# Relative attention of an eight-layer kernel: heads in pairs, values weighed in column strips, the mask inside the row maximum

## The reference

```python
q, k, v = (split_head(xn @ W) for W in (Wq, Wk, Wv))          # 16 heads of 8
scores  = q @ k^T / sqrt(8) + skew(q @ rel_embed^T)           # 512 x 512 a head
scores  = where(causal, scores, -inf)
out     = softmax(scores) @ v                                 # 512 x 8 a head
y       = merge_heads(out) @ Wp + bp
```

## Time and profile before

| | us |
|---|---|
| median of 3 runs | 4825.27 |
| lowest, highest | 4806.19, 4838.93 |
| profiled execution | 4821.89 |
| its span, first to last instruction | 4820.2 |

### The profile page before, as it was taken

How to read it: one execution, slowest core, us unless ns; L and a number is a source line. 1 busy time by engine, 2 the same in 40 slices (tenths; PEclk the granted TensorE clock), 3 DMA queues, 4 the chain that set the end, 5 groups by cost and what they waited for, 6 DMA issues and landing times.

```text
span 4820.2 us, 76474 instructions
## 1 busy us (share of the span) xinstructions
PE 4323.8 (90%) x30051; PEld 2656.8 (55%) x30051; DVE 2385.6 (49%) x6922; ACT 1718.7 (36%) x3496; POOL 841.7 (17%) x1441
## 2 busy tenths in 40 slices
PE   7988989889898898988989889898898988988989
PEld 3556645565455654556545565455654556545575
DVE  3435644365443654436544365443654446544455
ACT  2333533334333343333433334333343333433334
POOL 2003111031110311103011040110401104011140
PEclk8999999999899999999989999999998999999989
DMA  2000000000000000000000000000000000000000
GB/s 70 1 1 1 1 6 1 1 1 1 6 1 1 1 1 6 1 1 1 1 6 1 1 1 1 6 1 1 2 1 6 1 1 2 1 4 1 1 1 3
DMA packets 19714, 17.25 MB, mean 4 GB/s; under 512 B 2605, under 2 KB 18942, under 8 KB 19326
## 3 DMA queue, kind: packets, MB, share of 16 engines
q1 hardware_dynamic: 19325, 11.99, 0.9%
HBM read 9.89 MB, written 2.10 MB: 2 GB/s over the span
## 4 chain that ended last, share of the span: by engine, by line
PE 79%; DVE 7%; POOL 7%; ACT 4%; issue 3%; DVEq 0%; POOLq 0%; ACTq 0%; SPq 0%
PE banks L987 7%; PE banks L991 7%; PE banks L977 7%; PE banks L884 7%; PE banks L827 6%; PE banks L912 6%; POOL work L480 4%; PE banks L924 3%; PE banks L869 3%; PE banks L1184 3%; PE banks L1205 3%; PE banks L1171 2%; PE banks L1077 2%; PE banks L1112 2%; PE banks L1026 2%
## 5 line engine op out<-in xcount | busy, mean ns | idle before, releaser
L1373 DVE CUSTOM_DVE_ANT_0 work<-banks,mask_row 128x512 f32<-128x512 f32 (+3 forms) x1024 | 452.0, 488 | 269.5 <-PE banks L884 265.5
L884 PE MATMUL banks<-work 32*128 32x512 f32 (+3 forms) x2048 | 524.0, 488 | 11.4 <-DVE work L1373 11.4
L912 PE MATMUL banks<-work 32*128 32x256 f32 (+3 forms) x2048 | 503.9, 493 | 20.8 <-ACT work L640 20.8
L640 ACT ACTIVATE work<-banks 128x384 f32<-128x384 f32 (+1 forms) x768 | 368.9, 527 | 430.9 <-PE banks L912 428.4
L439 POOL TENSOR_TENSOR rstd<-rstd,half 128x2 f32<-128x2 f32 x128 | 87.3, 701 | 2377.0 <-DVE moments L1301 1802.9
L656 ACT ACTIVATE work<-banks 128x512 f32<-128x512 f32 (+1 forms) x384 | 228.6, 595 | 685.0 <-PE banks L987 684.8
L1446 DVE TENSOR_TENSOR work<-work,banks 128x512 f32<-128x512 f32 (+1 forms) x384 | 263.5, 686 | 343.0 <-PE banks L991 343.0
L987 PE MATMUL banks<-xnT,wg 128*128 128x512 f32 (+1 forms) x768 | 416.0, 624 | 0.0
L991 PE MATMUL banks<-xnT,wu 128*128 128x512 f32 (+1 forms) x768 | 406.4, 612 | 0.0
L449 POOL TENSOR_SCALAR_AFFINE_SELECT work<-work 128x128 f32<-128x128 f32 (+1 forms) x768 | 251.2, 330 | 884.4 <-ACT work L640 873.6
L977 PEld LDWEIGHTS banks<-wd,work 128*128 128x128 f32 (+1 forms) x3072 | 360.6, 191 | 57.3 <-issue 57.3
(11 more groups left out here) (254 smaller groups left out, 6992.3 us busy)
## 6 DMA issues: line engine op xcount, KB each, us to landing
x_next<-in_L_attn_a_x_dram SPq DMA_DIRECT2D x8, 256.0 KB, 2.9
out_dram<-x SPq DMA_DIRECT2D x8, 256.0 KB, 2.5
wg<-in_L_ffn_Wg_dram SPq DMA_DIRECT2D x1, 1376.0 KB
wu<-in_L_ffn_Wu_dram SPq DMA_DIRECT2D x1, 1376.0 KB
wd<-in_L_ffn_Wd_dram SPq DMA_DIRECT2D x2, 512.0 KB
wk_l<-in_L_attn_a_Wk_dram SPq DMA_DIRECT2D x1, 512.0 KB, 7.3
wv_l<-in_L_attn_a_Wv_dram SPq DMA_DIRECT2D x1, 512.0 KB, 6.8
wq_l<-in_L_attn_a_Wq_dram SPq DMA_DIRECT2D x1, 512.0 KB, 7.7
```

The lines of the kernel that those rows point to most:

```text
L640: eng.activation(prob4[:, G % 2, hh, C_AT[j]:C_AT[j] + C_N[j]], bank(3 + c % 3)[:, 0:C_N[j]], ACT.Exp).then_inc(s_exp, 1)
L884: m = eng.matmul(bank(k % 3)[:, col:col + N], q4[own, G, P * t:P * t + P], k4[own, G, 0:N], start=True, stop=True)
L912: m = eng.matmul(bank(3 + c % 3)[:, col:col + N], k4[own, G, P * s:P * s + P], q4[own, G, P * s:T], start=True, stop=True)
L1373: m = eng.tensor_tensor_reduce(out=summed[:, k % 2, col:col + N], in0=bank(k % 3)[:, col:col + N], in1=mask_row[:, T - N:T], scale=1.0, sc ...
```

## The change

- **Pairs.** The loop runs over `PAIRS` = 8 pairs of heads. `qk(p, j)` makes job j of heads 2p and 2p+1, head by head in turn for each product, into banks 0 and 1; it waits until both sums of the job before are done. The products with `mask_kq` are gone.
- **Mask.** `row_max` adds `mask_row` and takes the maximum in one instruction (the form of L1373), which also writes the masked rows into `r_prob`, now three places (`RING`). A further instruction negates the four maxima of a head and waits for the last of them. `exps` waits for that, reads and writes `r_prob`, and no longer reads PSUM.
- **Columns.** ScalarE copies all three column jobs, and into the head's own blocks of `sc`. `r_probT` is gone.
- **Values.** `weigh(G)` weighs the four heads of a group at once in strips of 32 stationary columns; it comes in every second pair from pair 4 on and once after the loop. `group_rows` and `heads_out` come in the pair after it, in bank 7.
- **Unread products.** `fill` issues products of 512 bf16 columns whose result nobody reads: nine after the projection, four ahead of the first scores, ten, four, six and four in pairs 0 and 1.

```diff
+        RING = 3
+        r_prob, _ = part(ring_at, [RING, COLS])
+        sc, at = part(ring_at + 4 * COLS, [H, len(BLOCKS), P])
...
-        ROW_JOBS = [(3, 2, 0), (2, 3, 0), (0, 3, 3 * P), (1, 4, 0)]
+        ROW_JOBS = [(3, 2, 0), (2, 3, 0), (0, 4, 2 * P), (1, 4, 0)]
+        ROW_AT = {0: 0, 1: P, 2: 3 * P, 3: 6 * P}
+        PAIRS = H // 2
...
             def exps(h):
-                at = {0: 0, 1: P, 2: 3 * P, 3: 6 * P}
-                if h >= 2:
-                    eng.wait_ge(r_pT, 3 * (h - 1))
-                for n, (t, bk, col) in enumerate(ROW_JOBS):
-                    eng.wait_ge(r_max, 4 * h + (3 if n == 1 else n + 1))
-                    eng.activation(r_prob[:, h % 2, at[t]:at[t] + (t + 1) * P],
-                                   bank(bk)[:, col:col + (t + 1) * P], ACT.Exp,
-                                   bias=r_neg_max[:, h % 2, t:t + 1]).then_inc(r_p, 1)
+                eng.wait_ge(r_neg, h + 1)
+                for t, _, _ in ROW_JOBS:
+                    v = r_prob[:, h % RING, ROW_AT[t]:ROW_AT[t] + (t + 1) * P]
+                    eng.activation(v, v, ACT.Exp, bias=r_neg_max[:, h % RING, t:t + 1]).then_inc(r_p, 1)
 
             def columns(h):
-                for j in range(2):
+                own = sc[:, h, :, :].rearrange("p b i -> p (b i)")
+                for j in range(3):
                     eng.wait_ge(r_pT, 3 * h + j + 1)
...
-            for i in range(1, H + 3):
-                if i - 3 >= G4 and (i - 3) % G4 == 0:
-                    group_columns(eng, 2, (i - 3) // G4 - 1, 7)
-                if 2 <= i <= H + 1:
-                    columns(i - 2)
-                if i <= H:
-                    exps(i - 1)
+            for i in range(1, PAIRS + 2):
+                if i >= 2:
+                    exps(2 * i - 3)
+                    columns(2 * i - 4)
+                if i <= PAIRS:
+                    exps(2 * i - 2)
+                if i >= 2:
+                    columns(2 * i - 3)
+                if i >= 4 and i % 2 == 0:
+                    group_columns(eng, 2, i // 2 - 2, 7)
...
+        def fill(eng, bk, count):
+            moving = relT[:, :, :].rearrange("p a b -> p (a b)")[:, 0:T]
+            for _ in range(count):
+                eng.matmul(bank(bk), identb[:, :], moving, start=True, stop=True)
...
         def pe_rel(eng, w):
             pe_project(eng, w)
+            fill(eng, 3, 9)
...
-            def qk(h, j):
+            def qk(p, j):
+                k = 3 * p + j
+                if k >= 1:
+                    eng.wait_ge(r_sum, 2 * k)
...
+                    fill(eng, 7, 4)
...
                 for s in JOBS[j]:
                     N = T - P * s
-                    eng.matmul(bank(k % 2)[:, col:col + N], stacked(k_st, h, slice(P * s, P * s + P)),
-                               stacked(q_st, h, slice(P * s, T)), start=True, stop=False)
-                    m = eng.matmul(bank(k % 2)[:, col:col + P], identb[:, :], mask_kq[:, :],
-                                   start=False, stop=True)
+                    for r in range(2):
+                        m = eng.matmul(bank(r)[:, col:col + N], stacked(k_st, 2 * p + r, slice(P * s, P * s + P)),
+                                       stacked(q_st, 2 * p + r, slice(P * s, T)), start=True, stop=True)
                     col += N
...
             def rows(h):
-                eng.wait_ge(r_sum, 3 * (h + 1))
+                eng.wait_ge(r_sum, 6 * (h // 2 + 1))
                 for i, (t, bk, col) in enumerate(ROW_JOBS):
-                    if h >= 1 and i != 2:
-                        eng.wait_ge(r_p, 4 * (h - 1) + (1, 3, 3, 4)[i])
+                    if h >= 1 and i < 3:
+                        eng.wait_ge(r_max, 4 * (h - 1) + (1, 2, 4)[i])
...
+            def columns(h):
+                for j in range(3):
+                    k = 3 * h + j
+                    if j == 0:
+                        eng.wait_ge(r_p, 4 * (h + 1))
+                    if k >= 2:
+                        eng.wait_ge(r_pTa, k - 1)
...
+            def weigh(G):
+                eng.wait_ge(r_pTa, 3 * G4 * (G + 1))
+                if G >= 1:
+                    eng.wait_ge(a_o, 2 * NG + G)
+                for s in range(NT):
+                    at = SLOT[(s, s)]
+                    for hh in range(G4):
+                        h = G4 * G + hh
+                        m = eng.matmul(bank(7)[32 * hh:32 * hh + 32, P * s:T],
+                                       val_row[:, s, BELOW * h:BELOW * h + 32],
+                                       sc[:, h, at:at + NT - s, :].rearrange("p b i -> p (b i)"),
+                                       start=(s == 0), stop=(s == NT - 1))
+                m.then_inc(a_pv, 1)
+
+            for i in range(PAIRS + 2):
+                if i < PAIRS:
+                    qk(i, 0)
+                if i >= 5 and i % 2 == 1:
+                    group_rows(eng, 2, (i - 5) // 2, 7)
+                if 1 <= i <= PAIRS:
+                    rows(2 * i - 2)
+                if i < 2:
+                    fill(eng, 7, (10, 4)[i])
+                if i < PAIRS:
+                    qk(i, 1)
+                if i < 2:
+                    fill(eng, 7, (6, 4)[i])
+                if i >= 2:
+                    columns(2 * i - 4)
+                if 1 <= i <= PAIRS:
+                    rows(2 * i - 1)
+                if i < PAIRS:
+                    qk(i, 2)
+                if i >= 4 and i % 2 == 0:
+                    weigh(i // 2 - 2)
+                if i >= 2:
+                    columns(2 * i - 3)
+            weigh(NG - 1)
...
-                def row_max(h):
-                    for i, (t, bk, col) in enumerate(ROW_JOBS):
-                        eng.wait_ge(r_sT, 3 * h + (1, 2, 2, 3)[i])
-                        eng.tensor_reduce(r_neg_max[:, h % 2, t:t + 1], bank(bk)[:, col:col + (t + 1) * P], AX.X,
-                                          ALU.max, negate=True).then_inc(r_max, 1)
+                def row_max(h, jobs):
+                    for i in jobs:
...
+                        if h >= RING and i == 0:
+                            eng.wait_ge(r_pT, 3 * (h - RING + 1))
+                        eng.tensor_tensor_reduce(out=r_prob[:, h % RING, ROW_AT[t]:ROW_AT[t] + N],
+                                                 in0=bank(bk)[:, col:col + N], in1=mask_row[:, T - N:T],
+                                                 scale=1.0, scalar=MASKED, op0=ALU.add, op1=ALU.max,
+                                                 accum_out=r_neg_max[:, h % RING, t:t + 1]).then_inc(r_max, 1)
+                    if jobs[-1] == 3:
+                        eng.wait_ge(r_max, 4 * (h + 1))
+                        eng.tensor_scalar(r_neg_max[:, h % RING, :], r_neg_max[:, h % RING, :], -1.0, None,
+                                          ALU.mult).then_inc(r_neg, 1)
+                for i in range(PAIRS + 2):
+                    if i < PAIRS:
+                        add(i, 0)
+                    if 1 <= i <= PAIRS:
+                        row_max(2 * i - 2, (0, 1, 2, 3))
+                    if i >= 5 and i % 2 == 1:
+                        heads_out(2, (i - 5) // 2, 7, r_rden)
+                    if i < PAIRS:
+                        add(i, 1)
+                    if 1 <= i <= PAIRS:
+                        row_max(2 * i - 1, (0, 1))
+                    if i < PAIRS:
+                        add(i, 2)
+                    if 1 <= i <= PAIRS:
+                        row_max(2 * i - 1, (2, 3))
```

106 lines of the change are left out of this document (22 added, 84 removed).

## The result

The changed kernel takes 4640.7 us in the median of four runs (4627.9 to 4657.4), the kernel before 4821.2 in four (4806.2 to 4838.9): ratio 0.963, interval 0.960 to 0.966. That is 3.7% faster. The profiled execution took 4628.8 us with a span of 4627.1: 193 us less than before, where the sum had said 210.

A forecast was written before the change was run, and what follows sets the result against it. TensorE alone was taken to bound the relative attention's head loop; strips, no mask products and paired scores save 26.2 us a turn, 210 in eight: 4821.9 - 210 = 4612, plus 3 for the median, 4615 us, range 4555 to 4685.

The forecast's parts named there:

- the sum: Whole kernel: head loop 26.2 us less a turn, 210 in eight; 4821.9 - 210 = 4612, plus 3 for the median.
- What bounds the kernel before, and what the strips give: Relative attention's head loop, 105.6 us: only TensorE's work counts; strips replace 9.0 us per four heads by 2.6.
- Row halves side by side: Score products of two heads overlap on row halves 0 and 64: 0.35, 0.45, 0.25 us for a pair's three jobs.
- The rival without overlap: Row halves don't overlap, each pair of score products costs double: 3.7 us a turn, 30 us, 4645; chance 0.18.
- The schedule: Head loop by pairs: 7.1 us each in pairs 2 and 3, then 9.4 with a weighing, 8.15 in the pair after.
- Negation: New VectorE instruction per head after the masked maxima: 0.25 us with its wait, bounds 0.1 and 0.55.
- VectorE becomes the bound, 7.1 us a pair: Head loop after the change: VectorE's sums, maxima and negations set the pace, except where `weigh` comes.
- Two signs of the prediction: Head loop: VectorE busy in eight tenths or more; the forecast is wrong if VectorE idles in every pair.
- Unread products: nothing for the nine, and the upper clock level for the loop, worth 3 us a turn: After the projection and at the first heads: fills hidden in waits; lower clock would cost some 3 us a turn.
- TensorE nowhere last: Head loop: copies and weighing cheaper than scheduled, VectorE's 7.1 + 7.7 hold for two pairs; 4560 us, chance 0.12.
- The clock low in the whole loop: Head loop: TensorE waits oftener, runs at 1.2 GHz and its work doubles; loop 120 us, total 4940, chance 0.06.
- Strips one after another: Weighing: strips don't run side by side, a group costs its 9.0 us again, nothing won; 4820 us, chance 0.04.

The follow-up runs named there:

- experiment 1: Kernel before with only the weighing in strips (own column blocks, four heads weighed at once): 4609.2 us, ratio 0.956.
- experiment 3: Changed kernel with the mask products back, eight to a pair, each behind its score product: 4748.6 us, ratio 0.987 to the kernel before.
- experiment 2: Changed kernel without any of its unread products: 4589.2 us, ratio 0.954 to the kernel before.
- experiment 4: Changed kernel with the weighing behind the next pair's first scores, `group_columns` and `group_rows` moved later too: 4579.9 us, ratio 0.952 to the kernel before.
- experiment 6: Changed kernel with two VectorE memsets at each turn's end, which turned out hidden: 4644.4 us, ratio 0.965 to the kernel before.
- experiment 7: Changed kernel without unread products, with two VectorE memsets at each turn's end, hidden likewise: 4600.1 us, ratio 0.955 to the kernel before.
- experiment 8: Changed kernel without unread products, with five VectorE memsets at each turn's end, really adding 0.6 to 1.2 us: 4612.6 us, ratio 0.957 to the kernel before.
- experiment 9: Changed kernel without unread products and with the weighing behind the next pair's first scores: 4596.7 us, ratio 0.955 to the kernel before.
- experiment 5: Changed kernel measured once more, unaltered: 4634.1 us, ratio 0.962 to the kernel before.

## Why the prediction was right, and where it was off

**What bounds the kernel before, and what the strips give.** Right. TensorE alone set the 105.6 us, and the weighing carries nearly all of the gain: experiment 1 has 23.8 of 27.9 us a turn. The taken size, 2.6 us, was 2.3.

**Row halves side by side.** Right: 0.32, 0.32 and 0.21 us for the three jobs of a pair, where 0.35, 0.45 and 0.25 were taken. The rival without overlap is refuted by the trace, and experiment 3 shows what ends the overlap. (The prediction's price for it was rough: its own terms, 2 x 0.66 + 2 x 0.25 + 1.5, give 3.3 us a turn and not 3.7, and two products one after the other could have cost as little as 2 x 0.22 us.) The Trainium skill (TensorEngine Tiling (Array Packing), Key Properties) says that changing the tiling mode drains the engine. Experiment 3 agrees as far as it goes: with a mask product behind each, the two 512-column scores cost what they cost one after the other, 0.62 us, and each of them 0.09 more than a full product in a dense row.

**The schedule.** Right, term by term. From the first sums to the last negation of pair 1: 12.2 forecast, 11.4 measured. Then 7.1 and 7.1: 7.00 and 7.01. With a weighing 9.4: 9.12. The pair after 8.15: 7.95. Drain 16.3: 16.4 (from 554.4, 7.95 behind 546.47, to 570.8). The loop 79.4: 77.5. Of the difference of 1.9 us, 0.75 are in the first two pairs and 0.96 in the four with weighings. (Four heads took 25.3 us before, from the weighing at 519.21 to that at 544.47, and not 24.9; the sum did not use this.) Negation: 0.25 forecast, under 0.2 measured.

**VectorE becomes the bound, 7.1 us a pair.** The number is right, the reading only half. In pairs 2 and 3 VectorE is nearly full, 6.75 and 6.76 of 7.0 us. But TensorE is as long there: 6.18 us busy, and 0.25 and 0.43 in which it must wait for ScalarE's copies. Experiment 3 put 2.06 us of TensorE's work into each pair and got 1.87 back, though VectorE had no more to do. In a pair, the sums must wait for the scores, the next scores for the sums, the maxima for `rows`, the last transposes for ScalarE's copy: a chain that goes through three engines. The loop's chain says so too: VectorE has 12 of its 77.5 us, ScalarE twice as much. Two signs of the prediction missed with it: VectorE busy in eight tenths of the loop or more (it is 56.0 of 77.5), and VectorE idle in every pair as a sign of being wrong, which is met, though with 0.18 us only in pairs 2 and 3.

**Unread products: nothing for the nine, and the upper clock level for the loop, worth 3 us a turn.** The clock was as said, 1.00 from the first sums on. Its worth was oversized: 0.6 us in the first pairs, 0.9 in the layer (experiment 2), since at either level VectorE's sums and maxima set the pace of those two pairs (in experiment 2 TensorE waits 2.33, 1.39, 0.85 and 1.00 us for its sums there). That step counted TensorE's longer transposes as if they lay on the path.

**The sum.** The range holds the result, and the forecast is 26 us off. The step that failed is its silence on the other layers: 4821.9 - 210 took everything outside the loop as fixed. The relative layer gained 223, the causal attentions lost 32. What they lost it to is the granted clock, 0.50 in a stretch where it can be 1.00. For the profiled execution the sum gave 4612 and 4628.8 were measured: 13 us too little gain counted in the loop, 32 us of loss not counted, 2 elsewhere. The other 9 of the 26 us are the median, which stands 12 above the profiled execution and not 3. The two traces of this kernel show its turns in another order of lengths; that the same makes its single times differ is likely, not shown. The earlier trace rows had shown the clock at the lower level in a stretch where TensorE was busy 1.47 of 2 us, so with waits of about a third of the work, where the prediction called them as long as the work; that it differs from turn to turn in code that was not touched could have been seen in the trace of before, where the first attention takes 78.3 in one turn and 80.8 in the next.

**What decides it, is in part open.** The traces of the eleven executions that leave these attentions as they are (before, after twice, experiments 1 to 4 and 6 to 9, with 176 causal attentions) sort them by one thing, how far into the attention the granted clock rises from the lower level that it has around the attention's start:

```
clock rises        attention takes   at the lower level again, us into it   how many
4.13 to 4.41 us    80.8 to 81.0      21 to 32, from 76 on                   39
4.42 to 5.39       87.8 to 88.2      22 to 36, 66 to 80, from 83 on         12
5.44 to 5.46       83.6              23 to 36, from 77 on                    2
5.48 to 5.71       85.5              23 to 30, 64 to 77, from 81 on          9
6.21 to 6.71       80.6 to 80.9      23 to 30, from 74 on                   22
6.75 to 7.38       78.1 to 78.4      not at all                             88
```

(In four of them the clock is up at the start already; they take 78.2, 78.4 and twice 80.8.) A tenth of a microsecond of difference in that moment can go with 3 to 7 us in the attention, with and without unread products. This is an order found in the traces. Experiment 8 is the one run that moved the moment on purpose, and it got the length that belongs to it. That the unread products are the cause of the loss is not shown. Without them most attentions are short (experiments 1, 2, 7, 9), but with them and the later weighing they are nearly as short (experiment 4), and the same kernel gives another order of lengths in another execution (experiment 5). Not tried was each of the six groups of unread products by itself.

**The other rivals.** TensorE nowhere last: false, the 2.29 us before the sums at 529.40. The clock low in the whole loop: false, 1.00 in its row, although TensorE pauses two or three times a pair. Strips one after another: false, four heads in 2.29 us.

## What to carry to other kernels

When a part is bound by one engine, take the largest block of that engine's work and look for a form in which several of its small products run side by side; here one such block gave 24 of 28 us a turn. Once the bound is gone, don't take the fullest engine alone for the next bound: here VectorE was busy 6.76 of 7.01 us, and 2.06 us more on TensorE still showed nearly in full, because TensorE's own work and its waits for the other engines added up to the same length. And sum a change over all stages of the trace after, not only the one that was edited: the clock in an unchanged stage came out differently after the change, and unread products put in to hold the clock have to be measured in the total.
